# Eight experts on one TensorE: order of the products, of the turned rows and of the loads

## The reference, cut to what matters

```python
capacity = max(1, int(T * CAPACITY_FACTOR / E))
...
keep = (rank <= capacity).astype(x.dtype) * onehot
w = jnp.einsum('tk,tke->te', topv, keep)
h = jax.nn.gelu(jnp.einsum('td,edf->etf', xt, W1) + b1[:, None, :], approximate=False)
y = jnp.einsum('etf,efd->etd', h, W2) + b2[:, None, :]
out = jnp.einsum('te,etd->td', w, y)
```

## Time and profile before

| | us |
|---|---|
| median of three runs | 655.75 |
| lowest, highest | 653.44, 655.78 |
| the profiled execution | 655.89 |
| its span, first to last instruction | 654.2 |
| granted TensorE clock, mean over the span | 0.958 |
| PE busy in the span | 581.0 (89%) |

### The profile page before, as it was taken

One profiled execution on the slowest core, in us unless ns is written; L12 is line 12 of the kernel. 1 busy time (PEld: TensorE's weight loads), 2 busy tenths in 40 slices (PEclk: granted clock), 3 DMA queues, 4 the chain that ended last, 5 costly groups with the idle time before them and its releaser, 6 DMA issues.

```text
span 654.2 us, 9424 instructions
## 1 busy us (share of the span) xinstructions
PE 581.0 (89%) x3411; PEld 442.0 (68%) x3411; DVE 407.3 (62%) x966; ACT 326.4 (50%) x567; POOL 172.3 (26%) x185
## 2 busy tenths in 40 slices
PE   7889989999998469999549598899999999998997
PEld 3556556556665259899536476688778878786866
DVE  6768778788884522543248986983769556762430
ACT  5756556566656115656216244752575256643351
POOL 5112122442543630000058623611300041001100
PEclk9989999999999679999859898999999999998999
DMA  4772242243110445844111100100000000000000
GB/s 130 228 251 94 84 130 62 85 145 97 53 46 2 132 143 172 258 113 125 42 30 33 28 6 1 33 1 0 1 18 0 1 1 18 0 1 2 17 1 16
DMA packets 44926, 42.51 MB, mean 65 GB/s; under 512 B 4176, under 2 KB 34384, under 8 KB 44880
## 3 DMA queue, kind: packets, MB, share of 16 engines
q1 hardware_dynamic: 42544, 37.44, 19.0%
q0 software_dynamic: 2048, 4.20, 2.2%
q10 hardware_dynamic: 288, 0.28, 0.3%
HBM read 25.12 MB, written 16.78 MB: 64 GB/s over the span
## 4 chain that ended last, share of the span: by engine, by line
PE 66%; DVE 10%; ACT 6%; issue 6%; DMA 5%; POOL 4%; SPq 2%; DVEq 0%; ACTq 0%; POOLq 0%
PE ps L1975 7%; PE ps L1641 6%; PE ps L1928 5%; PE ps L1657 5%; PE ps L1997 5%; PE ps L1669 5%; PE ps L1998 4%; PE ps L2078 4%; PE ps L2074 4%; PE ps L2075 4%; PE ps L2001 4%; PE ps L1991 2%; DMA XS<-xs_dram 2%; PE ps L1644 2%; POOL xs_dram L534 1%
## 5 line engine op out<-in xcount | busy, mean ns | idle before, releaser
L681 ACT ACTIVATE PT<-ps 128x384 f32<-128x384 f32 (+1 forms) x192 | 93.5, 529 | 71.2 <-PE ps L1657 68.9
L1070 DVE TENSOR_REDUCE pm<-ps 128x4 f32<-128x512 f32 x160 | 102.4, 681 | 11.1 <-PE ps L1641 10.4
L1641 PE MATMUL ps<-KP,QS 128*128 128x512 f32 x160 | 71.9, 454 | 7.8 <-DVEq L1063 2.5
L548 POOL TENSOR_SCALAR_AFFINE_SELECT PT<-PT 128x512 f32<-128x512 f32 x64 | 39.9, 636 | 129.8 <-ACT PT L681 129.7
L1657 PE MATMUL ps<-QM,KP 128*128 128x512 f32 (+3 forms) x256 | 69.5, 332 | 1.5 <-DVE QM L1084 1.1
L1657 PEld LDWEIGHTS ps<-QM,KP 128*128 128x128 f32 x256 | 44.3, 191 | 22.8 <-issue 12.6
L1641 PEld LDWEIGHTS ps<-KP,QS 128*128 128x128 f32 x160 | 29.9, 189 | 28.0 <-DVE pm L1070 11.6
L1440 DVE TENSOR_TENSOR_SCAN zero<-decay,OG 128x512 f32<-128x512 f32 x32 | 44.8, 1401 | 1.1
L1669 PE MATMUL ps<-PT,V 128*32 128x128 f32 (+3 forms) x512 | 45.2, 446 | 0.0
L523 POOL TENSOR_TENSOR rstd<-veps,mhalf 128x4 f32<-128x4 f32 x11 | 12.7, 1157 | 111.1 <-DVE veps L981 110.9
L1928 PE MATMUL ps<-W,HT 128*128 128x128 f32 x320 | 37.5, 277 | 3.2 <-issue 3.2
(11 more groups left out here) (308 smaller groups left out, 1386.1 us busy)
## 6 DMA issues: line engine op xcount, KB each, us to landing
qk_dram<-HL SPq DMA_DIRECT2D x24, 256.0 KB, 4.1
W<-in_eW SPq DMA_DIRECT2D x16, 256.0 KB, 3.6
QS<-qk_dram SPq DMA_DIRECT2D x15, 256.0 KB, 3.5
KP<-qk_dram SPq DMA_DIRECT2D x60, 64.0 KB, 2.5
xs_dram<-zero SPq DMA_DIRECT2D x4, 640.0 KB, 3.3
XS<-xs_dram SPq DMA_DIRECT2D x8, 320.0 KB, 4.9
ys_dram<-zero SPq DMA_DIRECT2D x8, 320.0 KB, 2.9
whole_h_w<-in_h_w SPq DMA_DIRECT2D x2, 1024.0 KB, 8.9
```

What stands on the lines that cost most here:

```text
L548: g.affine_select(out=diag, in_=diag, pattern=[[0, 4], [1, P]], compare_op=ALU.is_ge, fill=0.0, base=0, channel_multiplier=-1).then_inc(se ...
L681: act.activation(PT[:, i, a:z], bank[ROWB + n % KEYB][:, 0:z - a], ACT.Exp, scale=float(DK) ** -0.5).then_inc(exp_done, 1)
L1070: v.tensor_reduce(pm[:, t, k, :], bank[n % ROWB].rearrange("p (i n) -> p i n", n=P), AXX, ALU.max).then_inc(row_free[n % ROWB], 1)
L1641: mm = pe.matmul(to, QS[:, G % 2, t * P:(t + 1) * P], KP[:, G % 3, k, :, :].rearrange("p i n -> p (i n)"), start=True, stop=t != k)
```

## The change

The change reorders work; it removes none, and adds 12 products that nobody reads.

- PE: the products of an expert become chunk 0, chunk 1, the turned rows of the next expert, chunk 2, second products of chunk 0, chunk 3, second products of chunks 1, 2 and 3. Each group of second products (ten of the profile's matmuls) waits for the GELU of its own chunk. The result banks 4 and 5 now collect chunk by chunk, with the chunk outside and the block of rows inside.
- ACT: `round_rows(x + 1)` moves ahead of the fourth GELU. DVE: `store_rows(x + 1)` moves ahead of `low_weights(x + 1)`.
- PE ahead of expert 0: 25 spare products in place of 20, and 7 more behind the turned rows.
- SP: two of the wide weights are loaded before the loop; the other two in pass 0, the narrow ones in pass 1, the square ones in pass 2 (before: all wide ones ahead, narrow in pass 0, square in pass 1). The wide weights get a second semaphore for it.

```diff
-            for n in wide:
+            for n in wide[0:2]:
                 load_whole(n, 0)
             for x in range(E):
...
                 if x == 0:
+                    for n in wide[2:4]:
+                        load_whole(n, 3)
+                if x == 1:
                     for n in narrow:
                         load_whole(n, 1)
-                if x == 1:
+                if x == 2:
                     for n in square:
                         load_whole(n, 2)
...
+                    if f == 2 and x + 1 < E:
+                        round_rows(x + 1)
                 if x + 1 < E:
                     round_weights(x + 1)
-                    round_rows(x + 1)
                 if x in (1, 2):
                     for n in wide[2 * x - 2:2 * x]:
-                        split_flat(n, 0, len(wide))
+                        split_flat(n, (0, 3)[x - 1], 2)
...
                 if x + 1 < E:
+                    store_rows(x + 1, 1 - x % 2)
                     low_weights(x + 1, 1 - x % 2)
-                    store_rows(x + 1, 1 - x % 2)
...
-                for f in range(FF):
+
+                def hidden_products(f):
                     pe.wait_ge(h_done, x * FF + f + 1)
...
                     mm.then_inc(h_full, 1)
+
+                def row_products(f):
+                    pe.wait_ge(h_done, x * FF + f + 3)
+                    for j in range(ST):
+                        mm = pe.matmul(bank[4 + j // 4][:, (j % 4) * P:(j % 4 + 1) * P], HT[:, s, f, j * P:(j + 1) * P],
+                                       W2[:, s, f, :], start=(f == 0 and j % 4 == 0), stop=(f == FF - 1),
+                                       skip_group_check=True)
+                    return mm
+
+                hidden_products(0)
+                hidden_products(1)
                 if following:
                     turn_rows(x + 1, 1 - s, n + s)
+                hidden_products(2)
                 pe.wait_ge(ew_in[s], n * 32)
-                pe.wait_ge(h_done, x * FF + FF + 2)
                 pe.wait_ge(y_done, x + 1)
-                for j in range(ST):
-                    for f in range(FF):
-                        mm = pe.matmul(bank[4 + j // 4][:, (j % 4) * P:(j % 4 + 1) * P], HT[:, s, f, j * P:(j + 1) * P],
-                                       W2[:, s, f, :], start=(f == 0), stop=(f == FF - 1))
-                mm.then_inc(y_full, 1)
+                row_products(0)
+                hidden_products(3)
+                row_products(1)
+                row_products(2)
+                row_products(3).then_inc(y_full, 1)
...
-            stay_awake(20)
+            stay_awake(25)
             turn_rows(0, 0, 1)
+            stay_awake(7)
```

More of the change, by code:

```diff
@@ L329, in build @@
         eb2_in = sem("eb2_in")
-        whole_in = [sem(f"whole_in{k}") for k in range(3)]
+        whole_in = [sem(f"whole_in{k}") for k in range(4)]
         w_high, w_low = sem("w_high"), sem("w_low")
```

## The result

The changed kernel took 651.39 us (median of four runs, 650.77 to 651.65), against 655.76 for the kernel before beside it: a ratio of 0.9939, with a 95% interval of 0.9912 to 0.9966. A second measurement on another chip gave 652.34 against 655.14, 0.9955 (0.9940 to 0.9969). The change makes the kernel faster by about half a per cent.

What follows compares the result with a forecast made beforehand. PE was taken to set the pace in the experts' stage. From 655.89 us, minus 8.7 for reordering and filling, plus 4.1 for late rows and 2.0 for the clock, gives 653.3, forecast 653.2; range 650.0 to 656.8.

Steps and rivals of the forecast that it cites:

- An expert of 8.62 us: PE, experts with a following one: first products 3.53, turned rows 0.55, second products 4.54; 0.82 less than 9.44.
- GELU wait: PE, first products: chunk 2 waits for the GELU of chunk 0; 0.28 us an expert to be saved.
- wait for the fourth GELU: PE, ahead of the second products: the profile's 0.39 us of issue, to be saved in each expert.
- refilling: PE, second products: refilling of the pipe within their 4.70 us; 0.16 us an expert to be saved.
- Rival (d): PE: each switch between first and second products costs 0.16 to 0.39 us; slower, 658.3 to 665.7 us; chance 0.08.
- Expert 7, 8.55: Last expert, which turns nothing: 3.53 + 0.28 + 4.54 + 0.2 = 8.55 us, against 9.66 today.
- Ahead of expert 0, 1.5 us: Added spare products on PE keep the clock full through expert 0, winning back 1.5 us.
- The wait for the rows of expert 5, 4.1 us: PE in expert 4: rows queued behind the square weights land 13.26 us after the send; wait 4.1, bounds 3 to 5.
- The other big loads "just pass": SP queue, passes 0 and 1: rows land at 10.0 and 9.4 against a need at 10.39; no wait, up to 0.5.
- rival (c): Gap of 5 us, two half-clock stretches, or filling ahead of expert 0 brings nothing: 655.1 to 656.6 us; chance 0.17.
- Weights landing at T + 5.9: Next expert's weights: ACT wants them at 6.35 us after an expert's start, halves over at 7.7, before 8.62; no wait.
- The clock behind the gap, 2.0 us: PE behind expert 4's wait: half clock costs 1.5 us for one stretch, 3.0 for two; 2.0 taken.

Runs made afterwards that it cites:

- rows first: Changed kernel with the rows of expert x+3 issued in pass x ahead of the big loads: 647.18 us, ratio to before 0.9878.
- no spares: Changed kernel with the old 20 spare products and none behind the turned rows, run twice: 654.94 us (0.9994), again 653.69 us (0.9988).
- old loads: Changed kernel with the load order of the kernel before: 653.05 us, ratio to before 0.9972.
- order only: Kernel before with only the new order on PE, ACT and DVE, old spare products and load order: 652.82 us, ratio 0.9963.
- the control: The kernel before run once more with no edit: 654.57 us, ratio to before 0.9995.
- late turn: Changed kernel with the turned rows moved back behind chunk 3 of the first products: 648.03 us, ratio to before 0.9893.
- weights first: Changed kernel with rows ahead of big loads, square weights split over passes 2 and 3, each pass's weights issued ahead of the result: 644.31 us, ratio 0.9844.
- spares only: Kernel before with 25 spare products in place of 20 and 7 more behind the turned rows: 653.80 us, ratio 0.9987.

## Why the prediction was right

The time fell inside the range, 1.8 us below the forecast of 653.2. The likeliest outcome by its chances, 0.56, was within 0.5% of before; the first measurement, 0.61% below, lies just past that, where 0.37 stood, and the second, 0.45%, within it. By its own steps:

- **An expert of 8.62 us.** Measured 8.52 to 8.53. The three terms, GELU wait, wait for the fourth GELU and refilling, all went. The second products are a little cheaper than their weight loads suggested (1.11 + 3.35 = 4.46 against 4.54). That is 0.7 us more over seven experts. Rival (d), that each switch costs, is out: the chain has no piece between any two groups.
- **Expert 7, 8.55.** Measured 8.50.
- **Ahead of expert 0, 1.5 us.** The mechanism is right, by the traces with and without spare products. The size is not one number: without them expert 0 lost 0 in one trace of the changed kernel and 2.6 in another, and 1.3 and 1.5 in the two of before.
- **The wait for the rows of expert 5, 4.1 us, landing 13.26 after its send.** Measured 3.9 of idling (the turned rows start 4.1 later than in an undisturbed expert), landing 283.21 - 270.06 = 13.15 after it. This was the central step, and rows first shows its cause.
- **The other big loads "just pass".** This step failed, in the direction that rival (c) named. The rows of expert 3 landed 262.07 - 251.84 = 10.2 after their send, not 8.8, and expert 2 lost 1.2 us. I had scaled from 768 KB at the bandwidth of the best stretch.
- **Weights landing at T + 5.9, both halves over 0.9 us before they are needed.** In expert 6 those of expert 7 were there only at T + 7.7 (307.54 - 299.86), and it lost 0.6. I gave that no term.
- **The clock behind the gap, 2.0 us.** Measured 1.3 to 1.7, one stretch. Six traces have this gap (changed twice, no spares twice, old loads, order only). If the late start of the turned rows is taken off what the expert took too long, the four with one stretch leave 1.3 to 1.6 us and the two with two (no spares again, old loads) 2.6 to 2.8. The prediction had named both cases, 1.5 and 3.0, and taken a value between.
- **Sum of the stage.** 68.9 + 4.1 + 2.0 = 75.0, measured 75.4. The gain of 2.6 was 2.2. That it is so near is in part luck: experts 2 and 6 took 1.6 us more than forecast, expert 4 0.8 less and the other five 0.4 less together.
- **What the sum didn't have** are the other 2.1 us of the profiled difference, outside the stage. Low stretches of the clock came and went there between all executions, in the control too, but that they make up just these 2.1 us is not shown. The forecast had priced one at 1.5 either way. In the second measurement of the changed kernel the whole gain was 2.8 us, near the 2.6, so part of the first 4.4 is likely such chance. Whether some of it goes by the change the runs leave open.

The rule of the Trainium skill that the prediction weighed (DMA: Bandwidth & Descriptors, Rules for kernel authors: issue early, wait late) held: late turn, which follows it, has a stage 4.8 us shorter than the changed kernel's. The wait that was left was 0.5 us, not the 2.3 that I had worked out: I had put the turn at T4 + 3.53 and not counted the ten second products ahead of it. But waiting late is not the better end. Where no load is late an expert takes 8.52 us with the early turn and 8.79 with the late one.

## What to carry to other kernels

Work that is moved earlier on an engine asks for its data earlier; count the distance from the load's issue to the new place of the wait, with all that stands ahead of it in the same queue, before counting what the move saves. Here the denser order with the spare products would have been worth 9.4 us (the stage of before, 77.6, against the 68.2 of weights first), and 6.6 of it went to two 320 KB loads behind 1 and 2 MB that nobody needed yet (1.2 us in expert 2, 5.4 in expert 4); issuing what is needed next ahead of what is big gave most of it back (6.0 us of the stage). In this kernel a wait of PE of some 4 us cost about 1.5 us more than itself, through the clock, and near 3 in two of six traces; sixteen spare products in the wait kept the clock up.

## What was not expected of the hardware

- Two idle pieces ahead of expert 0, the first of 1.3 to 2.5 us and the second of 1.8, with 0.8 of work between, brought the half clock in four of five executions; the fifth had pieces as short as those of before (1.39 and 1.78 against 1.33 and 1.78) and kept the full clock. Waits of 1.0 us alone did not lower it: neither in before nor in expert 2 of the changed kernel, where the granted clock stayed at 1.00. The place of the drop moved: in before it came 1.1 us into expert 0, in the control at its first product, and in the second trace of no spares 1.1 us ahead of it.
- At the half clock ten second products took 2.13 us and at full clock 1.11, a first product 0.27 and 0.147: the products that wait on their weight loads suffer as much as the others.
- A row load of 320 KB behind two loads of 1 MB took 10.2 to 11.0 us from issue to landing in the ten traces whose chain shows it (before and changed twice each, late turn, spares only, both of no spares, old loads, order only).
